# The second step of a vision transformer block: GpSimd's sum of rows before the pixel differences, embedding products between the minima

## The reference

```
patches = 196 patches of 16*16*3 = 768 values per image
h  = patches @ W.T + b + pos          # embedding, 256 channels
h  = concat(cls_tok, h)               # 197 tokens
h  = h + attention(layernorm(h))      # 16 heads of 16 channels
h  = h + experts(layernorm(h))        # 4 experts, 256 -> 1024 -> 256, relu
```

## Time and profile before

| | us |
|---|---|
| median of 3 runs | 3955.44 (3953.28 to 3957.28) |
| profiled execution, its own time | 3955.86 |
| its span, first to last instruction | 3954.1 |
| TensorE busy | 3882.5 |
| VectorE busy | 2815.0 |
| GpSimd busy | 2819.3 |
| ScalarE busy | 2379.7 |
| mean granted clock of TensorE (1 is the full rate) | 0.992 |

### The profile page before, as it was taken

How to read it: one execution, slowest core, us unless ns; L and a number is a source line. 1 busy time by engine, 2 the same in 40 slices (tenths; PEclk the granted TensorE clock), 3 DMA queues, 4 the chain that set the end, 5 groups by cost and what they waited for, 6 DMA issues and landing times.

```text
span 3954.1 us, 87144 instructions
## 1 busy us (share of the span) xinstructions
PE 3882.5 (98%) x30276; PEld 3411.0 (86%) x30276; DVE 2815.0 (71%) x4315; ACT 2379.7 (60%) x4388; POOL 2819.3 (71%) x3543
## 2 busy tenths in 40 slices
PE   6799999999999999999999999999999999999998
PEld 4688888888888888888888888888888888888887
DVE  5677777677777777777767776777777777767763
ACT  5555666655666555666556665556665566665562
POOL 5567777667777677776677776777776777766776
PEclk9899999999999999999999999999999999999999
DMA  7244454444444444444444444445444444444455
GB/s 243 72 135 139 127 143 136 141 137 127 139 142 135 143 137 126 139 138 136 143 134 136 137 137 137 140 124 146 141 133 140 139 127 141 136 143 125 132 151 140
DMA packets 776547, 545.57 MB, mean 138 GB/s; under 512 B 157624, under 2 KB 701752, under 8 KB 775096
## 3 DMA queue, kind: packets, MB, share of 16 engines
q1 hardware_dynamic: 771416, 539.70, 46.7%
q10 hardware_dynamic: 4704, 0.30, 0.1%
HBM read 518.48 MB, written 21.30 MB: 137 GB/s over the span
## 4 chain that ended last, share of the span: by engine, by line
PE 94%; POOL 2%; ACT 1%; issue 1%; DMA 1%; DVE 1%; SPq 0%; ACTq 0%; POOLq 0%; DVEq 0%
PE ps L1335 66%; PE ps L1434 5%; PE ps L1419 5%; PE ps L1448 5%; PE ps L1533 4%; PE ps L1542 3%; PE ps L1550 2%; PE ps L1331 1%; PE ps L1511 1%; PE ps L1517 1%; PE ps L1499 1%; PE ps L1523 1%; PE ps L1505 1%; DMA w_sums<-hT 0%; ACT probs L711 0%
## 5 line engine op out<-in xcount | busy, mean ns | idle before, releaser
L1335 PE MATMUL ps<-xn,w1s 128*128 128x197 f32 x4096 | 909.2, 343 | 4.9 <-ACT hT L676 2.6
L1335 PEld LDWEIGHTS ps<-xn,w1s 128*128 128x128 f32 x4096 | 676.2, 189 | 143.9 <-issue 132.4
L1335 PE MATMUL ps<-hT,w_s 128*128 128x197 f32 x4064 | 784.1, 330 | 7.6 <-issue 7.3
L970 DVE SCALAR_TENSOR_TENSOR probs<-probs,ps 99x788 f32<-99x788 f32 x512 | 483.0, 969 | 321.8 <-ACT probs L711 321.8
L1335 PEld LDWEIGHTS ps<-hT,w_s 128*128 128x128 f32 x4064 | 692.1, 190 | 9.6 <-issue 7.9
L568 POOL TENSOR_TENSOR hT<-hT 128x197 f32<-128x197 f32 x508 | 331.9, 653 | 511.1 <-ACT hT L691 507.6
L1335 PE MATMUL ps<-xt,w1s 128*128 128x197 f32 x3072 | 681.3, 330 | 3.3 <-ACT hT L682 1.7
L561 POOL TENSOR_SCALAR hT<-hT 128x394 f32<-128x394 f32 x512 | 641.8, 1254 | 18.3 <-DVE hT L1091 18.3
L1045 DVE TENSOR_REDUCE lows<-ps 99x8 f32<-99x1576 f32 (+1 forms) x256 | 460.2, 1799 | 222.7 <-PE ps L1434 222.6
L1335 PE MATMUL ps<-hT,w_a 128*128 128x197 f32 x3048 | 591.0, 329 | 0.2 <-DVE yw L1109 0.2
L1335 PEld LDWEIGHTS ps<-xt,w1s 128*128 128x128 f32 x3072 | 538.2, 190 | 36.1 <-DVE hT L1097 3.3
(11 more groups left out here) (142 smaller groups left out, 6229.7 us busy)
## 6 DMA issues: line engine op xcount, KB each, us to landing
w_s<-w_sums SPq DMA_DIRECT2D x508, 256.0 KB, 3.6
w_a<-in_w SPq DMA_DIRECT2D x384, 256.0 KB, 3.2
w1s<-w_sums SPq DMA_DIRECT2D x512, 192.0 KB, 2.6
w1s<-in_w SPq DMA_DIRECT2D x512, 128.0 KB, 2.3
x<-in_xT SPq DMA_DIRECT2D x30, 1188.0 KB, 7.1
w1s<-in_w SPq DMA_DIRECT2D x512, 64.0 KB, 2.0
w1s<-w_sums SPq DMA_DIRECT2D x512, 64.0 KB, 2.0
out_rows<-rows SPq DMA_DIRECT2D x252, 48.0 KB
```

The costliest lines, as they stand in the source:

```text
L970: nc.vector.scalar_tensor_tensor(out=part, in0=part, scalar=3.75, in1=ps[0:HB, 2 * half:2 * half + 2, 0:N], op0=ALU.add, op1=ALU.mult).the ...
L1335: return mm(place, weights, rows, start=start, stop=True, skip_group_check=True)
```

## The change

On GpSimd, the four pixel differences of pair 2 move from s = 3 of step 0 to behind `sum_h2(0)` (the first two) and behind `sum_squares2(0)` (the other two). On ScalarE, `squares2(0)` moves ahead of the second v copy, and `gate_product(0)` behind two of the three embedding copies. On VectorE, `zb_of(0)` moves ahead of the last minimum. On TensorE, `mean2(0)` and the fourth minimum's product move ahead of the second v projection; the first transposes move behind the fifth minimum's product; and the five embedding products move from the end of the step to between the minima's products: product 0 before `lowest(1, 5)`, 1 and 2 before `lowest(1, 6)`, 3 and 4 before `lowest(1, 7)`. No operation is added or removed, and no size changes.

```diff
--- before.py
+++ after.py
@@ -623,14 +623,15 @@
                         for e in range(E):
                             weight_sums(e)
                         embed_weight_sums()
-                        for i in range(4):
-                            pixel_sums(2, i)
                     if s in (6, 7, 9, 10) and pair > 0 and pair + 2 < PAIRS:
                         pixel_sums(pair + 2, (6, 7, 9, 10).index(s))
                     if s == 11 and has_b:
                         sum_h2(b)
                     if s == 13 and has_b:
                         sum_squares2(b)
+                    if s in (11, 13) and pair == 0:
+                        for i in (s - 11, s - 10):
+                            pixel_sums(2, i)
                     if s == 15 and has_b:
                         token_sums(b)
                     x = n * E + s // 4 - 1
@@ -840,12 +841,12 @@
                 q_of(1, 1, 1)
                 halves(0, 3)
                 v_of(1, 0)
+                squares2(0)
                 v_of(1, 1)
-                squares2(0)
                 rs2_of(0, True)
-                gate_product(0)
                 emb_p1(2)
                 emb_v(2)
+                gate_product(0)
                 emb_x(2)
 
             def step(pair, has_b, has_f, has_n, has_t):
@@ -1204,8 +1205,8 @@
                 low(1, 5)
                 gate_sum(0)
                 low(1, 6)
+                zb_of(0)
                 low(1, 7)
-                zb_of(0)
                 q_max_of(1, 1)
                 emb_sums_2(2)
 
@@ -1620,20 +1621,22 @@
                 project_out(0, 1, (q_ready, at(1, 4, 4)))
                 lowest(1, 2, (low_ready, at(1, 8, 2)))
                 project_v(1, 0, (k_ready, at(1, 4, 4)))
-                project_v(1, 1, (whole_ready, 8))
                 mean2(0)
                 lowest(1, 3, (low_ready, at(1, 8, 3)))
+                project_v(1, 1, (whole_ready, 8))
                 variance2(0)
-                lows_to_columns(1, 0, (low_ready, at(1, 8, 4)), (v_ready, at(1, 2, 2)))
-                lowest(1, 4)
+                lowest(1, 4, (low_ready, at(1, 8, 4)))
+                lows_to_columns(1, 0, (v_ready, at(1, 2, 2)))
+                embed_product(2, 0)
                 lowest(1, 5, (low_ready, at(1, 8, 5)))
+                embed_product(2, 1)
+                embed_product(2, 2)
                 lowest(1, 6, (low_ready, at(1, 8, 6)))
                 gate_logit(0)
+                embed_product(2, 3)
+                embed_product(2, 4)
                 lowest(1, 7, (low_ready, at(1, 8, 7)))
                 lows_to_columns(1, 1, (low_ready, at(1, 8, 8)), (q_max_ready, at(1, 4, 2)))
-                embed_product(2, 0, (v_ready, at(1, 2, 2)))
-                for k in range(1, 5):
-                    embed_product(2, k)
 
             def step(pair, has_b, has_f, has_n, has_t):
                 if pair == -1:
```

## The result

The changed kernel takes 3940.10 us in the median (3939.26 to 3945.54, 6 runs), the kernel before 3955.43 (3953.28 to 3958.67, 6 runs): a ratio of 0.9961, 95% interval 0.9951 to 0.9972. That is 15.3 us saved, where 18.2 were forecast (3937.2, range 3933 to 3946.5).

A forecast was written before the change was run, and what follows sets the result against it. TensorE, 98% busy, was taken to bound the whole span, the change touching only waits in the second step. A first gap product 19.2 us earlier, less 1.0 in step 1, gave 18.2 saved: 3937.2 us, range 3933 to 3946.5.

The forecast's parts named there:

- Step 1, the sum ahead of the pixels: GpSimd, second step: the sum of rows runs at 99.93 before the pixel differences, so the mean comes 5.5 us earlier.
- 1 us to spare: GpSimd's sum of squares could stand a pixel landing up to 1 us late before being held by it.
- Steps 2 to 5, the layout: Second step from variance to q_max: embedding products at 1.16 between minima, first gap product at 123.85, 19.2 us earlier.
- the sign: VectorE in the second step: expected to run without a hole from 107.5 to 115.
- Step 6, what step 1 makes of it: Start of step 1 on TensorE: 1.0 us taken off for a short clock fall after two idle holes, leaving 18.2.
- third rival: Start of step 1: the clock's fall is carried in and makes the kernel slower; 3964 us, chance 0.02.
- The half clock inside the new stretch: Second step: TensorE stays at the lower clock, in part or throughout; 3943 or 3946 us, chance 0.33.
- lost on the way to the end: Behind step 1: a later fixed event, such as a transfer, takes back over 11 us; 3955 us, chance 0.05.

The follow-up runs named there:

- v_first: The changed kernel with the second v projection ahead of the mean again and the second v copy ahead of the squares; 3941.0 us in the median.
- product4_last: The changed kernel with embedding product 4 behind the last minimum's product instead of ahead of it; 3938.0 us in the median.
- filled_hole: The changed kernel with one useless matmul pair added on TensorE behind the last minimum's product; 3936.4 us in the median.

## Why the prediction was right, and where it was off

**Step 1, the sum ahead of the pixels.** Right. The sum starts 0.08 behind h2, in every trace of that order, and takes 1.02. The mean's place in the queue matters (v_first, 2.1 us of distance). The forecast's "1 us to spare" for a late landing was thin: in one of the traces it was used up.

**Steps 2 to 5, the layout.** The sum gave 23.97 us from h2 to the first gap product; measured were 23.35, twice. The embedding products cost 1.16 to 1.27 and not 2.34, as chosen. The product of low 7 was held 0.9 by products 3 and 4 where I had 1.4. The three early products were hidden: VectorE works from 112.59 to 120.41 without a wait, as the sign named.

**The start.** The sum set h2 at 99.88, from one trace. Over the twelve traces, in all of which the work ahead is the same, it is 101.6 in the mean and 99.9 to 105.1 at the ends, since TensorE's clock falls at other places each time. In the kernel before, an early or late h2 was hidden behind the pixels' wait; in the changed one it is passed on in full. So the gain measured from an execution with an early h2 was 1.7 us too large, of which a landing that is 0.7 later than in that trace in the mean (five traces in which it shows: 100.3, 100.8, 101.6, 102.3, 102.8) gives some back.

**Step 6, what step 1 makes of it: the term that was mis-sized.** I took off 1.0 for "one short fall of the clock there, about 3 us". The clock was at 0.51 for 6.8 us, and it cost 2.9. By the third rival's own price, 0.35 us for each us at half the clock, 6.8 us would make 2.4, so the length of the fall was the larger part of the error. The 2.9 is read as follows: the second gap product starts 7.79 behind the first (136.28), against 4.86 in product4_last. The whole of it was avoidable, as filled_hole shows. The changed kernel has about 1 us more at the very end: from its last second layernorm to the end of the span it takes 133.5 and 133.7 us in its two traces, and the kernel before 132.4 and 131.1. Over all twelve traces that part takes 130.7 to 133.8, with the clock down at different places. Why is open, and no term of the sum stood for it.

The corrected sum: 19.2, plus 0.6 for the shorter distance, less 1.7 and plus 0.7 for h2 and the landing, less 2.9, is 15.9, and 14.7 with 1.2 less for the end of the span; measured were 15.3 and 13.8. That the forecast of 18.2 missed by only 3 to 4 us owes a little to luck: the distance was priced 0.6 too long, and a later landing gave back 0.7. The profiled execution: 19.2 plus 0.6, less 5.3 for its h2, less 2.9, less 1.2 at the end, is 10.4, its span's difference.

**The rivals.** The half clock inside the new stretch did not come in the changed kernel (1.00 in 104 to 128), nor did the lower level reach far into step 1. The clock did fall within such a stretch in product4_last and v_first, so the rival was near. The page of the Trainium skill cited for it, TensorE: Matmul & The Clock Gate, section on psum-queue depth-cycling, describes swings of the clock from short idles between groups; in the changed kernel the swing came at the last two holes alone, though 1.58 us of idle stood ahead of low 6's product with the clock at 1.00 behind it (0.93 for that product), and filling one of the last two removed it. No gain was lost on the way to the end but for the 1 us above.

## What to carry to other kernels

A step that is taken off a wait inherits the scatter of what it follows: price it from where its input is ready in several executions, not in one. Where independent work can be put into holes of the bounding engine, put it where the holes are longest, the last one ahead of the dense stretch first: here the place of one product of 1.2 us was worth more than its own length (2.1 and 3.1 us between the medians of product4_last and of the changed kernel). When a move is priced, ask for TensorE both what it hides and which holes it leaves.

## What the runs showed of the hardware

A matmul pair of no use, 0.93 us in a 1.9 us hole, took 2.9 us off the start of step 1, by the granted clock (products of 1.16 instead of 2.17, where the clock had been 0.51 for 6.8 us). The granted clock ahead of the change differs between executions of the same program (0.66 in 40 to 44 us in one trace of the changed kernel, 1.00 in the other, and 0.50 and 0.70 in 60 to 76), and with it the time of h2 by 3.6 us; over all twelve traces h2 varies by 5.3. The third token sum on GpSimd took 2.45 us in the changed kernel too, and the sum of rows 1.02, so that one instruction is slow and the sum that moved is not; why it is slow was not tested.
